# Linear attention and a mixture of experts on one core: the last chunks of attention put in an order written out by hand

## What is computed

```
xn = layernorm(x)
q, k, v = split(xn @ w_attn.T)            # 16 heads of 16
y  = causal linear attention over chunks of 128 tokens, phi = elu + 1
attn = y @ w_proj.T
logits = xn @ gate_w.T + gate_b + expert_bias
e = argmax(logits)                        # one of 8 experts for each token
ffn = relu(xn @ w1[e] + b1[e]) @ w2[e] + b2[e]
out = x + attn + ffn
```

## Time and profile before

| | before |
|---|---|
| median of three runs | 514.45 us (513.82 to 514.84) |
| the profiled execution, its own time | 514.6 us |
| its span | 512.8 us |
| TensorE busy, share of the span | 94% |
| VectorE busy | 79% |
| ScalarE busy | 55% |
| GpSimd busy | 51% |
| mean granted clock of TensorE | 0.984 |

### The profile page before, as it was taken

How to read it: one execution, slowest core, us unless ns; L and a number is a source line. 1 busy time by engine, 2 the same in 40 slices (tenths; PEclk the granted TensorE clock), 3 DMA queues, 4 the chain that set the end, 5 groups by cost and what they waited for, 6 DMA issues and landing times.

```text
span 512.8 us, 17442 instructions
## 1 busy us (share of the span) xinstructions
PE 479.5 (94%) x6067; PEld 393.1 (77%) x6067; DVE 406.6 (79%) x881; ACT 280.6 (55%) x537; POOL 259.5 (51%) x469
## 2 busy tenths in 40 slices
PE   1899999999999999999987599999999999999996
PEld 0678887888878888788864488888888888888884
DVE  3788999999999999999878377777777777776775
ACT  3448887788877888877875033333333333333331
POOL 4345667667667676676664523343343343333222
PEclk9999999999999999999999699999999999999998
DMA  8524565665655665655441522122212212210000
GB/s 254 202 65 139 184 204 155 188 206 173 190 179 171 190 201 171 193 177 177 138 159 63 184 57 79 56 82 75 65 54 71 79 58 76 71 49 28 24 15 1
DMA packets 34304, 62.88 MB, mean 123 GB/s; under 512 B 5677, under 2 KB 10030, under 8 KB 34096
## 3 DMA queue, kind: packets, MB, share of 16 engines
q1 hardware_dynamic: 29232, 49.17, 30.4%
q0 software_dynamic: 4992, 12.60, 8.1%
HBM read 51.00 MB, written 13.50 MB: 126 GB/s over the span
## 4 chain that ended last, share of the span: by engine, by line
PE 82%; DVE 5%; POOL 4%; issue 4%; ACT 3%; DMA 1%; DVEq 0%; POOLq 0%; ACTq 0%
PE ps L612 21%; PE ps L625 20%; PE ps L385 7%; PE ps L427 6%; PE ps L456 5%; PE ps L497 5%; PE ps L470 4%; PE ps L440 3%; PE ps L403 3%; PE ps L483 2%; PE ps L581 2%; PE ps L410 1%; PE ps L489 1%; PE ps L368 1%; DVE AR L664 1%
## 5 line engine op out<-in xcount | busy, mean ns | idle before, releaser
L612 PEld LDWEIGHTS ps<-AR,W 128*128 x1872 | 131.5, 99 | 40.0 <-issue 1.1
L612 PE MATMUL ps<-AR,W 128*128 128x128 f16 x1872 | 155.6, 221 | 0.9 <-ACT AR L1165 0.9
L625 PE MATMUL ps<-W,ST 128*128 x624 | 150.4, 326 | 0.0
L1174 ACT ACTIVATE ST<-ST 128x512 f16<-128x512 f32 x78 | 49.2, 630 | 116.3 <-DVE ST L1003 116.3
L1322 POOL DMA_INDIRECT out<-AR x39 | 39.5, 1013 | 118.6 <-DVE AR L1035 116.5
L1003 DVE SCALAR_TENSOR_TENSOR ST<-ps,TAs,B1S 128x512 f32<-128x512 f32 x78 | 58.6, 751 | 48.3 <-PE ps L612 48.3
L1261 POOL TENSOR_TENSOR W<-ST,W 128x512 f16<-128x512 f32 x64 | 74.2, 1160 | 28.9 <-ACT W L1117 28.3
L720 DVE TENSOR_TENSOR AR<-ps,CT 128x512 f32<-128x512 f32 x128 | 82.0, 683 | 3.9 <-PE ps L427 3.9
L1015 DVE SCALAR_TENSOR_TENSOR ST<-ST 128x512 f16<-128x512 f32 x78 | 53.6, 687 | 15.6 <-ACT ST L1174 15.6
L385 PE MATMUL ps<-xT,WA 128*128 128x128 f16 x768 | 50.7, 225 | 5.0 <-ACT xT L1067 2.7
L1317 POOL DMA_INDIRECT AR<-scr,AR x39 | 40.1, 1029 | 29.5 <-issue 21.6
(11 more groups left out here) (145 smaller groups left out, 757.9 us busy)
## 6 DMA issues: line engine op xcount, KB each, us to landing
ST<-in_w SPq DMA_DIRECT2D x128, 256.0 KB, 4.1
scr<-XR SPq DMA_DIRECT2D x32, 256.0 KB, 2.1
XR<-in_x SPq DMA_DIRECT2D x32, 128.0 KB, 4.6
AR<-in_b SPq DMA_DIRECT2D x1, 1024.0 KB, 4.8
AR<-in_wall SPq DMA_DIRECT2D x2, 388.0 KB, 4.1
AR<-scr,AR POOLq DMA_INDIRECT x39, 3.4
out<-AR POOLq DMA_INDIRECT x39, 2.5
ST<-in_cst SPq DMA_DIRECT2D x1, 576.0 KB, 5.2
```

The source lines that it names most:

```text
L612: a = e.matmul(dst, W[:, off:off + 57472][:, bass.ds(place_of(s), 128)], XT16[s % 2][:, xl * 256 + k * 128:xl * 256 + (k + 1) * 128], star ...
L625: a = e.matmul(PS[4 + s % 2][:, 0:w], src[h % 4][:, fs], W[:, off:off + 57344 + w][:, bass.ds(place_of(s), w)], start=(f == 0 and w == 512 ...
L1174: e.activation(HH[h % 4], H32[h % 2], ACT.Relu).then_inc(a_hh, 1)
```

## The change

- **Banks.** For the last chunk (31) the scores of r = 0 go to PS[0] and no longer to PS[2], and `yt1`, `yt2`, `pr` and `res` use PS[3]. `scores(31)` waits for `kt(31)` in place of `res(29)`, and `yt1(31)` waits for the mask of PS[3] in place of `res(30)`.
- **Order.** The loops of TensorE and VectorE end after period 32, and what followed is written out.
- **Routing.** `pick_a`, `pick_b`, `pick_c` and `ahead` of the last group stand between the masks of chunk 31. `places(0)` and `places(1)` stand in period 32 before `res(28)`, `places(2)` before `res(30)`.
- **Weights.** From period 32 on there are five quarters in a period and no longer three. The third and later quarters of a period come after `y2`, `relu` and `exp` on ScalarE.

The core of the diff:

```diff
+        def psc(c, r):
+            return PS[0] if c == NC - 1 and r == 0 else PSC[r]
+        def py(c):
+            return PS[3] if c == NC - 1 else PS[2]
...
-            return range(min(2 * (NC - 5) + 3 * (p - NC), NW), min(2 * (NC - 5) + 3 * (p - NC) + 3, NW))
+            return range(min(2 * (NC - 5) + 5 * (p - NC), NW), min(2 * (NC - 5) + 5 * (p - NC) + 5, NW))
...
-                if c >= 2:
+                if c == NC - 1:
+                    e.wait_ge(S["kt"], NC)
+                elif c >= 2:
                     e.wait_ge(S["res"], c - 1)
...
-                e.wait_ge(s_[0], min(c + 2, NC))
-                if c >= 1:
-                    e.wait_ge(S["res"], c)
+                if c == NC - 1:
+                    e.wait_ge(s_[1], NC)
+                else:
+                    e.wait_ge(s_[0], min(c + 2, NC - 1))
+                    if c >= 1:
+                        e.wait_ge(S["res"], c)
...
-            for p in range(NC + 5):
+            for p in range(NC + 1):
                 if on(p - 3):
                     scores(p - 3)
...
+            scores(NC - 2)
+            st(NC - 2)
+            ktr(NC - 1)
+            yt1(NC - 3)
+            inter(NC - 2)
+            yt2(NC - 3)
+            scores(NC - 1)
+            pr(NC - 3)
+            pv(NC - 2)
+            yt1(NC - 2)
+            place(3)
+            inter(NC - 1)
+            yt2(NC - 2)
+            pv(NC - 1)
+            pr(NC - 2)
+            yt1(NC - 1)
+            yt2(NC - 1)
+            pr(NC - 1)
...
-            for p in range(NC + 3):
+            for p in range(NC + 1):
                 if on(p - 2):
                     phi(p - 2)
...
-                if p == NC + 1:
-                    pick_a(3)
-                    pick_b()
-                    pick_c(3)
-                if p == NC + 2:
-                    bases()
+                if p == NC:
+                    places(0)
+                    places(1)
                 if on(p - 4):
                     res(p - 4)
...
+            phi(NC - 1)
+            s_mask(NC - 2, 0)
+            s_mask(NC - 2, 1)
+            y(NC - 3)
+            s_mask(NC - 2, 2)
+            s_mask(NC - 2, 3)
+            t32(NC - 2)
+            pick_a(3)
+            s_mask(NC - 1, 0)
+            s_mask(NC - 1, 1)
+            pick_b()
+            res(NC - 3)
+            s_mask(NC - 1, 2)
+            s_mask(NC - 1, 3)
+            pick_c(3)
+            ahead(3)
+            y(NC - 2)
+            bases()
+            own(3)
+            own_sum(3)
+            own_slot(3)
+            first_slots()
+            places(2)
+            res(NC - 2)
             y(NC - 1)
             to_slots()
             res(NC - 1)
-            places(2)
             places(3)
...
-                for n in q[1:]:
+                for n in q[1:2]:
                     w_scale(n)
                     w_hi(n)
...
+                for n in q[2:]:
+                    w_scale(n)
+                    w_hi(n)
```

More of the change, by code:

```diff
@@ L426, in scores @@
                         rows = slice(32 * r, 32 * r + 32)
-                        a = e.matmul(PSC[r][:, g * 256:(g + 1) * 256], QK[c % 2][rows, 256 + g * 128:384 + g * 128],
+                        a = e.matmul(psc(c, r)[:, g * 256:(g + 1) * 256], QK[c % 2][rows, 256 + g * 128:384 + g * 128],
                                      QM[c % 2][rows, g], start=True, stop=True)
@@ L488, in yt2 @@
                 for k in range(2):
-                    a = e.transpose(PS[2][:, k * 128:(k + 1) * 128], Y32[:, k * 128:(k + 1) * 128], ID32)
+                    a = e.transpose(py(c)[:, k * 128:(k + 1) * 128], Y32[:, k * 128:(k + 1) * 128], ID32)
                 a.then_inc(S["yt2"], 1)
@@ L543, in tensor @@
                     place(eights(p, 13))
-                if p == NC + 2:
-                    place(3)
                 if p == 2:
@@ L732, in y @@
             def y(c):
-                o = PS[2][:, :].rearrange("p (h e) -> p h e", h=16)
+                o = py(c)[:, :].rearrange("p (h e) -> p h e", h=16)
                 d = DN[:, :].rearrange("p (h o) -> p h o", o=1)
@@ L747, in res @@
                 e.wait_ge(S["pr"], c + 1)
-                e.tensor_tensor(xb[:, 256:512], PS[2][:, 256:512], xb[:, 256:512], ALU.add).then_inc(S["res"], 1)
+                e.tensor_tensor(xb[:, 256:512], py(c)[:, 256:512], xb[:, 256:512], ALU.add).then_inc(S["res"], 1)
             def w_max(n):
@@ L955, in vector @@
                 w_max(2 * p + 1)
-                if p == NC + 1:
-                    ahead(3)
-                    places(0)
-                    places(1)
-                if p == NC + 2:
-                    own(3)
-                    own_sum(3)
-                    own_slot(3)
-                    first_slots()
+            phi(NC - 1)
[22 more added lines that the diff above has]
+            res(NC - 2)
             y(NC - 1)
@@ L1109, in y2 @@
                     e.wait_ge(S["pr"], c)
-                e.activation(YT2, PS[2][:, 0:256], ACT.Copy).then_inc(S["y2"], 1)
+                e.activation(YT2, py(c)[:, 0:256], ACT.Copy).then_inc(S["y2"], 1)
             def w_hi(n):
```

7 lines of the change are left out of this document (3 added, 4 removed).

## The result

The changed kernel takes **521.53 us**, the median of four runs (521.11 to 522.57), beside 514.64 us for the kernel before on the same chip. The ratio is 1.0138, with an interval of 1.0117 to 1.0159: slower by 6.9 us. The forecast was 519.2, slower by 4.7. The profiled execution took 521.11 us, its span is 519.3.

A forecast was written before the change was run, and what follows sets the result against it. TensorE was taken to bound up to 260 us, then a chain across engines for 21 us. Terms 4.0 - 0.8 + 1.2 + 0.4 = +4.8 us on the profiled 514.6 gave 519.4, median 519.2; range 517.0 to 521.5.

The forecast's parts named there:

- Two `places` in 1.26: VectorE, after C16 lands: places(0) and places(1) take 1.26 us ahead of res(28), within the stall term.
- the first half clock, +1.2: TensorE from scores(30) on: after idling in the stall it runs at 1.2 GHz, costing 1.2 us (bounds 0 and 2.5).
- the second half clock: TensorE after its second gap, while VectorE masks: the clock may fall again, costing 0.4 us (bounds 0 and 0.8).
- The stall, +4.0: VectorE waits 4.8 us for C16, queued behind the fifth load, so scores(30) starts 4.0 us later.
- The estimate from the Trainium skill: C16's transfer: 3.35 us for 576 KB by the skill's rule, giving 517.3; rejected for the measured 5.2 us.
- The stretch behind `pv(30)`, -0.8: VectorE without gaps from pv(30): index matmuls 20.1 us after scores(30) at full clock, not 20.91, a gain of 0.8.
- over 23: Sign on the stretch from scores(30) to the index matmuls: expected 21 to 22 us; under 20 or over 23 refutes the sum.
- The rest: ScalarE's five quarters a period and chunk 31's own banks: costed at nothing; without cover a quarter, up to 1.3 us.
- the rival without a stall: C16 in time but weights delay yt1(29) on ScalarE: index matmuls 0.5 us later, 515.0 us; 4%.
- C16 sooner: Rival: the table lands after 3.4 us, 1.8 us less stall, 517.4 us; 8%.
- The clock falls more than once and where it counts: Rival: two TensorE gaps bring both clock terms to their upper bounds, 1.7 us more, 520.9 us; 15%.
- Faster: Rival: C16 landed by 258.6, pr(29) no longer waits behind weights, TensorE's 1.75 us gap and half clock go: 513.3 us; 4%.

The follow-up runs named there:

- e3: Changed kernel with 48 extra matmuls, results unread, on TensorE in the stall before scores(30): 521.73 us, ratio 1.013.
- e7: Changed kernel with three quarters a period, all ahead of y2, and GpSimd's w_lo of quarters 60 to 62 held until ahead(3) is done: 517.09 us, 1.0028.
- e1: Changed kernel with the table C16 issued ahead of the last two of the five loads, behind three as before: 517.59 us, ratio 1.0061.
- e2: Changed kernel with places(0) and places(1) moved behind pick_a(3), the table left late in SyncE's queue: 517.47 us, ratio 1.0056.
- e12: Changed kernel with places(0), (1) behind pick_a(3) and, in chunk 31's masks, the wait for pv(30) ahead of that for scores(31): 519.04 us, 1.0057.
- e16: Changed kernel with three, five, one, one quarters, routing and places(0), (1) ahead of res(29), places(2) behind res(31), GpSimd's remainders held: 511.74 us, 0.9971.
- e4: Changed kernel with the weights part undone, three quarters a period and all ahead of y2 on ScalarE: 518.64 us, ratio 1.0078.

## Why the prediction was right in direction and short in size

The forecast was 519.2 us, and the measured 521.53 lies 2.3 above it and just above the range's end of 521.5. The mechanism was right: the table behind the fifth load, the stall, the half clock behind it. Two terms of the sum failed in size. "Two `places` in 1.26" took 2.05 beside GpSimd's subtractions, and "the first half clock, +1.2" was 2.2, of which e3 shows 1.95 to be the clock. Smaller terms were a later landing, a wait ahead of the masks, the second half clock and a wait for `pr(31)`. The index matmuls came 7.7 us later and not 4.8; the time rose by less, as the profiled execution was 1.09 us ahead at `scores(29)`.

**The stall, +4.0: right, and +5.4 in size.** Every link is in the trace. C16 was issued at 257.20, on before's scale (1.09 more) at 258.3 where 258.2 was put. It landed after 5.6 us, not 5.2. VectorE had 5.38 us of idle time. The estimate from the Trainium skill, "DMA: Bandwidth & Descriptors", section "Anatomy of one DMA — SWDGE (gpsimd) path", was 3.35 us; the measured 3.7 to 6.0 us of this transfer in the kernels of the study lie above it all. The term that failed was "two `places` in 1.26": they took 2.05, since the last remainder of GpSimd ended only at 263.81 (in e7 such steps took their usual time once the remainders were moved away), and so `res(28)` came 0.7 us later than by the sum. The row was there, has the slots' first comparison at 1.58 and the second at 0.81, the same size, and I did not ask why. Together the start was 1.4 us later than put. e1 and e2 confirm what the stall is worth: without it 4.1 us of the time.

**The first half clock, +1.2: too small.** `scores(31)` came 6.98 us after `scores(30)` and not 4.8 plus 1.2. e3 measures the term by itself at 1.95. The sum had put `scores` at 0.56 us, from the slow `scores(31)` of the earlier trace rows, and as much for what follows. But that row was at half clock only in part (0.69 from 270 to 272 us). Here `scores(30)` took 2.09 for 1.15, and the state matmuls, `ktr` and `yt1` behind it 1.27, 0.64 and 1.06 for 0.73, 0.38 and 0.63: 0.9 and 1.2 us more.

**The stretch behind `pv(30)`, -0.8: 0.1 less on VectorE, 0.5 more in a wait.** `y(30)` started 4.11 us after the masks of 31, 4.15 by the sum. But the masks themselves started 0.49 us after `pv(30)` had ended, where I had put nothing; e12 only leans to a cause.

**The second half clock, +0.4: 0.9.** VectorE waited 0.92 us before `res(30)`. After that the slots took 1.6 in place of 2.42, since the remainder that had lengthened them before was done, and instead the index matmuls waited for `pr(31)`, 0.4 us. Together 1.0 + 0.5 + 0.5 - 0.8 + 0.4, less the 0.1 on VectorE, is 1.5, which is the stretch of 23.2 us against the 21.7 of the sum. The text had named over 23 as what would prove the sum wrong, and it did.

**"The rest", nothing: wrong, and hidden.** This is the step that the experiments correct most, and the changed kernel by itself doesn't show it. Its weights were done in the stall. Take the stall away, as e1 does, and `yt1(29)` waits as the rival without a stall had it (3.53 us after `scores(30)`, 3.6 by its sum), but from there to the index matmuls it takes 20.98 us where that rival put 18.1. By e1's timelines the 2.9 are 1.6 at half clock ahead of `res(30)`, 0.9 in routing steps beside GpSimd's remainders (L849 took 1.09 us), 0.5 before the masks of 31, 0.3 on the way to `scores(31)`, less 0.3 in the slots. So the rival's 515.0 was 2.6 us too good: the rest of the change costs 0.6% even with the table in time, and e16 shows that an order written out by hand need not.

**The other rivals.** C16 sooner did not happen. "The clock falls more than once and where it counts" did: the two clock terms came to 3.1 us (2.2 and 0.92), where I had 1.6 and upper bounds of 3.3. Its 520.9 is the nearest of all the cases, and I had given it 15%; that it is so near is partly luck, since its stall was 1.4 us short and the earlier start of `scores(29)` hid 1.1. Faster did not happen. Its gap does go: `pr(29)` follows `scores(31)` without one in every kernel of the new order. That alone gains nothing, as e1 and e4 show; with the routing, the remainders and the last quarter moved too, in e16, the index matmuls come 2.6 us before those of the kernel before.

## To carry to other kernels

Before a step is moved ahead of another, ask for each thing it waits for in which queue that stands and behind what: here a table of 576 KB stood behind a load that could not go yet. Cost a small step on VectorE by its longest row as well as by its shortest, and look at what GpSimd does beside the place that it moves to; and before weights are moved on ScalarE, look for the copy behind them that waits for nothing but its turn. A stall hides what the same change costs elsewhere: after the cause is found, take it away and look again.
